# Two quads of value products in one turn, eight probability buffers, k over two turns, w_o and gate in one turn each

## The chip, the core and the metric

The kernel runs on one NeuronCore of one Trainium2 chip. The metric is device time in microseconds. The core has TensorE (PE in the profile; its weight loads are PEld), VectorE (DVE), ScalarE (ACT), GpSimd (POOL) and SyncE (SP), which here only issues DMAs.

## The reference

Sixteen sequences of 256 tokens by 256 features go through attention with 16 heads of 16 features, a layer norm over x plus attention, a mixture of 8 experts (two per token, capacity 1280 rows each, hidden size 1024) and a second layer norm:

```
q, k, v = x @ w.T, split in 16 heads
probs   = softmax(q k^T / 4)
x       = layernorm(x + (probs @ v) @ w_o.T)
gates   = softmax(x @ gating_w); top 2, weights normalised, dropped over capacity
x       = layernorm(x + sum over the two experts of weight * (relu(x @ w1 + b1) @ w2 + b2))
```

## The kernel before, in words

The program has three stages, one after the other: `attention` (lines 99 to 932), `experts` and `last_norm`. The change touches `attention` alone, which is the first 440 us or so.

In `attention` every engine walks the same list of turns, `for turn in range(LAST + 1)`, 182 of them. Each step has an offset in turns (lines 238 and 239), and `due(turn, offset, NB)` gives the sequence for which the step is due in this turn, if any; a sequence is started every 8 turns, so some seven sequences are in flight and a turn's content depends on turn mod 8, called its phase. `pair_of` gives the steps that are done in every turn, for one of the eight pairs of heads. Within a turn an engine does what is due in the order in which the code lists it, and waits on semaphores; nothing else keeps engines in step.

```
XT, Q, K, V, ST_IN, S0, MT, ST0, PV0 = 0, 2, 4, 8, 7, 12, 20, 23, 25
UT, AT, O, LN, X1, X1T, LG, CH, POS, LIST = 35, 37, 38, 41, 45, 46, 49, 54, 55, 59
```

TensorE (lines 822 to 932) does this in a turn, in this order: `scores` of a pair (line 787, four matmuls into the two banks SQ); `shifted_scores` of a pair (line 802, into SD); MT, transposes of the maxima; UT, eight transposes of unnormalised outputs (line 853); AT and X1T, transposes of attn and x1 (line 761); `pv` (line 818), the value products of one quad, that is four heads, with 128x32 tiles, sixteen matmul records; POS (lines 879 and 880); the q, k and v products, twelve matmuls each (helper line 752); O, the w_o product; LG, the gate product; XT, transposes of the next x. By phase, beside the eight matmuls of the two scores groups in each:

| phase | TensorE before |
|---|---|
| 0 | v product (12 matmuls), XT |
| 1 | one quad, half of the gate product (6) |
| 2 | q product (12), other half of the gate product (6) |
| 3 | UT, one quad |
| 4 | MT, k product (12) |
| 5 | AT, one quad |
| 6 | X1T, half of the w_o product (6) |
| 7 | one quad, POS, other half of the w_o product (6) |

VectorE's first work in a turn is the reduction of the scores to their negated maximum (line 672, `negm`); `scores` of the next turn waits for it, as SQ is held once. Behind it come, in the order of the code: `slots` (phase 0), `qk_lo` (line 570: q in phase 3, k in phase 5), `chosen` (lines 604 to 624, phase 6), layer norm statistics (phase 1), `heads_out` (lines 578 to 585, phase 3), mT_lo (phase 4), aT_lo (line 711, phase 5), y (line 718, phase 7), `largest` (lines 593 and 598, phase 2). ScalarE does first the exponential of a pair (line 488, `probs`), whose buffer is one of four; then by phase v_aug, mT_hi, x1 (line 519), aT_hi (line 526), x1T_f, `u_copy` of two quads (line 479, phases 3 and 7), xT_f and `qk_hi` (line 474: q in phase 2, k in phase 4). The w_o product waits for aT_lo (line 905).

The rows of q and k are then rearranged by six DMAs on SP's queue (lines 311 to 313) into `stack`, one of three buffers, from which `scores` reads from turn 12 of that sequence (phase 4) on. SP goes through its own list in order: in each sequence the four shift DMAs of line 291 (after mT_lo), two stores of x1 (lines 296 and 297, after x1), then the six of `stack`, after q_lo, k_lo and the use of that buffer three sequences back, then a load of x while there are sequences left. The scores of phase 4 wait for all six (line 782).

Before the turns, the weights are loaded into `w_raw` and transposed, and `ones_f` (two rows of ones) is copied into the stacks.

## Time and profile before

| | us |
|---|---|
| median of 3 runs | 980.37 |
| lowest and highest run | 977.14, 990.34 |
| the profiled execution, its own time | 981.65 |
| its span, first to last instruction | 979.8 |
| mean granted TensorE clock | 0.915 of full |
| PE, DVE, ACT, POOL busy in the span | 846.6, 561.8, 461.4, 431.8 |

Read it so: the time is that of the device, the span that of the profiled instructions, and all times of the rows below count from the span's start. Busy TensorE is an average over stages; what a turn costs is read from the starts of successive scores groups (line 787).

### The profile page before, as it was taken

The numbers are of one execution on the slowest core, as the hardware profiler recorded it, in microseconds if no ns is written. First come the engines' busy times: TensorE is split into PE (matmuls) and PEld (weight loads), VectorE is DVE, ScalarE is ACT, GpSimd is POOL, SyncE is SP. The second block draws the span as 40 slices with busy tenths as digits, with TensorE's granted clock in tenths as the row PEclk, the third lists the DMA queues.
The fourth block names the chain that finished last, engine by engine and source line by source line (L and its number), as shares of the span: only waits on it lengthen the run. The fifth ranks groups of instructions, "written<-read, shape, count | busy, mean of one in ns | idle before, by whom it ended". The sixth has DMA issues, their size and how long they took to land. (4 is left out here: it accounts for less than half of the span.)

```text
span 979.8 us, 19547 instructions
## 1 busy us (share of the span) xinstructions
PE 846.6 (86%) x7441; PEld 753.7 (77%) x7441; DVE 561.8 (57%) x1151; ACT 461.4 (47%) x851; POOL 431.8 (44%) x636
## 2 busy tenths in 40 slices
PE   5579889999999997840999999999999999999940
PEld 4466667677777765540999999999999999999940
DVE  3356647777777786241455666565555545666415
ACT  3036646666666665311344444444444444444316
POOL 2000215555656555474144545444444444545225
PEclk8579989999999999665899999999999999999985
DMA  5755967676775551014123444343442524322229
GB/s 127 101 80 79 246 126 117 106 119 115 116 113 97 90 108 28 23 44 152 34 45 87 88 91 87 48 95 84 93 87 43 130 45 86 87 44 46 26 35 334
DMA packets 74807, 90.75 MB, mean 93 GB/s; under 512 B 10428, under 2 KB 61788, under 8 KB 74588
## 3 DMA queue, kind: packets, MB, share of 16 engines
q1 hardware_dynamic: 57308, 68.47, 33.2%
q0 software_dynamic: 17408, 21.05, 13.2%
q8 instruction: 59, 0.97, 0.5%
q14 instruction: 32, 0.26, 0.1%
HBM read 37.87 MB, written 25.84 MB: 65 GB/s over the span
## 5 line engine op out<-in xcount | busy, mean ns | idle before, releaser
L1014 POOL DMA_INDIRECT acc_rows<-o_w,lists x80 | 136.5, 1706 | 242.0 <-ACT o_w L1065 229.8
L672 DVE TENSOR_REDUCE negm<-wide 128x4 f32<-128x1024 f32 x128 | 156.2, 1220 | 65.5 <-PE wide L787 65.3
L1143 PE MATMUL wide<-g_hi,w_hi 128*128 128x256 f32 x640 | 184.3, 288 | 0.0
L1145 PE MATMUL wide<-g_hi,w_lo 128*128 128x256 f32 x640 | 181.0, 283 | 0.0
L1144 PE MATMUL wide<-g_lo,w_hi 128*128 128x256 f32 x640 | 180.8, 282 | 0.0
L1162 PE MATMUL bank<-w_lo,h_hi 128*128 128x256 f32 x640 | 180.1, 281 | 0.0
L1161 PE MATMUL bank<-w_hi,h_hi 128*128 128x256 f32 x640 | 180.1, 281 | 0.0
L1163 PE MATMUL bank<-w_hi,h_lo 128*128 128x256 f32 x640 | 179.8, 281 | 0.0
L1055 ACT ACTIVATE h<-wide,b1T 128x256 f32<-128x256 f32 x320 | 132.9, 470 | 71.3 <-DVE h_hi L1098 53.2
L488 ACT ACTIVATE probs<-wide 128x1024 f32<-128x1024 f32 x128 | 131.0, 1024 | 74.0 <-PE wide L802 70.8
L1065 ACT ACTIVATE o_w<-o_b,lists 128x256 f32<-128x256 f32 x80 | 36.3, 502 | 193.6 <-DVE o_b L1111 193.6
L1143 PEld LDWEIGHTS wide<-g_hi,w_hi 128*128 128x128 f32 x640 | 121.5, 190 | 0.3 <-DVE g_lo L1088 0.3
L1144 PEld LDWEIGHTS wide<-g_lo,w_hi 128*128 128x128 f32 x640 | 121.6, 190 | 0.0
L1145 PEld LDWEIGHTS wide<-g_hi,w_lo 128*128 128x128 f32 x640 | 121.4, 190 | 0.0
L1161 PEld LDWEIGHTS bank<-w_hi,h_hi 128*128 128x128 f32 x640 | 120.5, 188 | 0.0
L1163 PEld LDWEIGHTS bank<-w_hi,h_lo 128*128 128x128 f32 x640 | 120.5, 188 | 0.0
L1162 PEld LDWEIGHTS bank<-w_lo,h_hi 128*128 128x128 f32 x640 | 120.4, 188 | 0.0
L1100 DVE TENSOR_TENSOR h_lo<-h,h_hi 128x512 fp32r<-128x512 f32 x160 | 110.7, 692 | 5.5
L1003 POOL DMA_INDIRECT rows<-x_rows,lists x80 | 88.2, 1102 | 33.2 <-issue 24.1
L1111 DVE TENSOR_TENSOR o_b<-bank,b_all 128x256 f32<-128x256 f32 x80 | 30.2, 419 | 113.9 <-PE bank L1163 113.9
L787 PE MATMUL wide<-stack 48*128 48x256 f32 x512 | 68.3, 347 | 25.2 <-DVE negm L672 16.0
L1098 DVE CAST h_hi<-h 128x512 fp32r<-128x512 f32 x160 | 70.1, 438 | 29.7 <-ACT h L1055 28.5
(162 smaller groups left out, 1510.4 us busy)
## 6 DMA issues: line engine op xcount, KB each, us to landing
stack<-qk SPq DMA_DIRECT2D x96, 256.0 KB, 8.1
w_raw<-in_L_ffn_w SPq DMA_DIRECT2D x16, 1024.0 KB, 5.9
x_sb<-in_L_attn_x SPq DMA_DIRECT2D x16, 256.0 KB, 8.6
x_rows<-x SPq DMA_DIRECT2D x16, 256.0 KB, 4.1
acc_rows<-x SPq DMA_DIRECT2D x16, 256.0 KB, 4.4
acc_sb<-acc_rows SPq DMA_DIRECT2D x8, 512.0 KB, 7.5
out<-out_sb SPq DMA_DIRECT2D x8, 512.0 KB, 3.7
x_rows<-zrow SPq DMA_DIRECT2D x1, 1280.0 KB, 11.8
```

The costliest lines, as they stand in the source:

```text
L488: nc.scalar.activation(probs[:, i % 4].rearrange("p x c t -> p x (c t)"), SD[:, :, :], ACT.Exp, scale=SCALE).then_inc(exp_done, 1)
L672: nc.vector.tensor_reduce(negm[n % 2][:, :, :, u].rearrange("p c x -> p x c"), SQ[:, :, :].rearrange("p x (c t) -> p x c t", c=QC), X, ALU ...
L1003: nc.gpsimd.indirect_dma_start(out=rows[c][:, r, :], out_offset=None, in_=x1_d, in_offset=bass.IndirectOffsetOnAxis(ap=lists[:, e, QC * c ...
L1014: nc.gpsimd.indirect_dma_start(out=acc_d, out_offset=bass.IndirectOffsetOnAxis(ap=lists[:, e, QC * c + r, 0:1], axis=0), in_=o_w[c][:, r, ...
L1055: ins = nc.scalar.activation(h[m % 2][:, i, :], bank(BZ[m], a=2)[:, i, :], ACT.Relu, bias=b1T[:, col:col + 1] if isinstance(col, int) else ...
L1100: nc.vector.tensor_tensor(h_lo[HBUF[c]][:, t, :], h[m % 2][:, :, :], h_hi[HBUF[c]][:, t, :].bitcast(F32), ALU.subtract).then_inc(h_lo_done, 1)
L1143: nc.tensor.matmul(out, w1_hi[:, k, f], G_hi[:, k, :], start=(k == 0), stop=False)
L1144: nc.tensor.matmul(out, w1_hi[:, k, f], G_lo[:, k, :], start=False, stop=False)
L1145: ins = nc.tensor.matmul(out, w1_lo[:, k, f], G_hi[:, k, :], start=False, stop=(k == DK - 1))
L1161: nc.tensor.matmul(out, H_hi[:, f, rs], w2_hi[:, f, :], start=(f == 0), stop=False)
L1162: nc.tensor.matmul(out, H_hi[:, f, rs], w2_lo[:, f, :], start=False, stop=False)
L1163: ins = nc.tensor.matmul(out, H_lo[:, f, rs], w2_hi[:, f, :], start=False, stop=(f == FT - 1))
```

## The change

It moves work between turns and makes `probs` larger. The value products of quads 0 and 1 are issued together in the turn in which quad 1 was due (phase 3), those of quads 2 and 3 in the turn of quad 3 (phase 7). `probs` gets eight buffers, one per pair, so the exponential of pair i waits for the value products of pair i - 8. The k product does its first six matmuls in phase 4 and the other six in phase 5; the ScalarE copy k_hi moves to phase 5 and the VectorE difference k_lo to phase 6. Both halves of the w_o product are issued in phase 6, both halves of the gate product in phase 1. The raw weights and the ones take no room of their own, they lie in buffers 4 to 7 of `probs`, which are first written by the exponentials of pairs 4 to 7. The number of instructions and all of their shapes stay.

```diff
--- before.py
+++ after.py
@@ -125,7 +125,10 @@
 
         tri = sb("tri", [P, P], BF16)
         ones = sb("ones", [P, P], BF16)
-        w_raw = sb("w_raw", [P, 4, DK, D])
+        probs = sb("probs", [P, PAIRS, 2, QC, S])
+        probs_flat = probs[:, :, :, :, :].rearrange("p u x c t -> p (u x c t)")
+        w_raw = probs_flat[:, 4 * 4 * S:4 * 4 * S + 4 * DK * D].rearrange("p (w c d) -> p w c d", w=4, c=DK)
+        ones_f = probs_flat[0:2, 6 * 4 * S:6 * 4 * S + PAIRS * S].rearrange("p (u t) -> p u t", u=PAIRS)
         wT_hi = sb("wT_hi", [P, 4, DK, D], F32R)
         wT_lo = sb("wT_lo", [P, 4, DK, D], F32R)
         b1_raw = sb("b1_raw", [NE * FT, P])
@@ -135,7 +138,6 @@
         iota_e = sb("iota_e", [P, NE])
         fill = sb("fill", [P, NE, BLK, 2], I32)
         zrow = sb("zrow", [P, D])
-        ones_f = sb("ones_f", [2, PAIRS, S])
         tok = sb("tok", [P, QC])
 
         x_sb = [sb(f"x_sb{i}", [P, QC, D]) for i in range(XB)]
@@ -149,7 +151,6 @@
         negm = [sb(f"negm{i}", [P, QC, 2, PAIRS]) for i in range(2)]
         mT_hi = sb("mT_hi", [H, S], F32R)
         mT_lo = sb("mT_lo", [H, S], F32R)
-        probs = sb("probs", [P, 4, 2, QC, S])
         u_sb = sb("u_sb", [P, QUADS, S])
         rec = sb("rec", [P, QC, H])
         attn = sb("attn", [P, QC, D])
@@ -483,9 +484,9 @@
                 if p is not None:
                     i = PAIRS * p[0] + p[1]
                     act.wait_ge(st_ready, i + 1)
-                    if i >= 4:
-                        act.wait_ge(pv_ready, (i - 4) // 2 + 1)
-                    nc.scalar.activation(probs[:, i % 4].rearrange("p x c t -> p x (c t)"), SD[:, :, :], ACT.Exp,
+                    if i >= PAIRS:
+                        act.wait_ge(pv_ready, (i - PAIRS) // 2 + 1)
+                    nc.scalar.activation(probs[:, i % PAIRS].rearrange("p x c t -> p x (c t)"), SD[:, :, :], ACT.Exp,
                                          scale=SCALE).then_inc(exp_done, 1)
                 m = due(turn, CH, NB)
                 if m is not None:
@@ -545,7 +546,7 @@
                 n = due(turn, Q, NB)
                 if n is not None:
                     qk_hi(n, 0, q_ready, q_hi_done)
-                n = due(turn, K, NB)
+                n = due(turn, K + 1, NB)
                 if n is not None:
                     qk_hi(n, 1, k_ready, k_hi_done)
 
@@ -681,7 +682,7 @@
                 n = due(turn, Q + 1, NB)
                 if n is not None:
                     qk_lo(n, 0, q_hi_done, q_lo_done)
-                n = due(turn, K + 1, NB)
+                n = due(turn, K + 2, NB)
                 if n is not None:
                     qk_lo(n, 1, k_hi_done, k_lo_done)
                 m = due(turn, CH, NB)
@@ -761,9 +762,9 @@
                         ins = nc.tensor.transpose(banks[bk][:, c * S + r * P:c * S + r * P + P], src[:, r, c * P:c * P + P], ident[:, :])
                 return ins
 
-            def by_feature_tile(w, n):
+            def by_feature_tile(w, n, tiles=range(G)):
                 hi, lo = xT_hi[n % 2], xT_lo[n % 2]
-                for o in range(G):
+                for o in tiles:
                     ins = product(banks[BC][:, o * S:o * S + S], split_pairs(
                         lambda i: wT_hi[:, w, i, o * P:o * P + P], lambda i: wT_lo[:, w, i, o * P:o * P + P],
                         lambda i: hi[:, i, :], lambda i: lo[:, i, :]))
@@ -815,7 +816,7 @@
                     for j in range(4):
                         u = 2 * t + j // 2
                         out = banks[BU][32 * j:32 * j + 32, (t % 2) * S:(t % 2) * S + S]
-                        ins = nc.tensor.matmul(out, v_aug[n % VB][:, c, 4 * t + j, :], probs[:, u % 4, j % 2, c, :],
+                        ins = nc.tensor.matmul(out, v_aug[n % VB][:, c, 4 * t + j, :], probs[:, u, j % 2, c, :],
                                                start=(c == 0), stop=(c == QC - 1), tile_position=(0, 32 * j))
                 ins.then_inc(pv_ready, 1)
 
@@ -865,10 +866,11 @@
                     pe.wait_ge(attn_done, min(m + 2, NB))
                     pe.wait_ge(x1T_lo_done, m)
                     transpose4(BB, x1[m % 2]).then_inc(x1T_ready, 1)
-                for t in range(QUADS):
-                    m = due(turn, PV0 + 2 * t, NB)
+                for half in range(2):
+                    m = due(turn, PV0 + 2 + 4 * half, NB)
                     if m is not None:
-                        pv(m, t)
+                        pv(m, 2 * half)
+                        pv(m, 2 * half + 1)
                 m = due(turn, POS, NB)
                 if m is not None:
                     pe.wait_ge(seen_done, m + 1)
@@ -888,7 +890,10 @@
                 if n is not None:
                     pe.wait_ge(q_lo_done, n + 1)
                     pe.wait_ge(wT_lo_done, 2)
-                    by_feature_tile(1, n).then_inc(k_ready, 1)
+                    by_feature_tile(1, n, (0,))
+                n = due(turn, K + 1, NB)
+                if n is not None:
+                    by_feature_tile(1, n, (1,)).then_inc(k_ready, 1)
                 n = due(turn, V, NB)
                 if n is not None:
                     if n >= 2:
@@ -904,11 +909,9 @@
                 if m is not None:
                     pe.wait_ge(aT_lo_done, m + 1)
                     by_row_tile(BA, aT_hi, aT_lo, 3, 0)
-                m = due(turn, O + 1, NB)
-                if m is not None:
                     by_row_tile(BA, aT_hi, aT_lo, 3, 1).then_inc(o_ready, 1)
                 for c in range(QC):
-                    m = due(turn, LG + c, NB)
+                    m = due(turn, LG, NB)
                     if m is not None:
                         if c == 0:
                             pe.wait_ge(x1T_lo_done, m + 1)
```

## Rows read from the trace of the kernel before

**Rows 1.** Windows view, 240 to 260 us: busy us (instructions) by engine, clock, DMA.
```profile
240.00:260.00 20.00, 18.98 (x192) 14.69 (x191) 14.88 (x31) 12.34 (x19) 11.79 (x28) 1.00 0.68 115
```

**Rows 2.** Timeline of TensorE: start, us, engine, line, operation, tiles, count [idle before <-releaser].
```profile
141.71 0.51 PE L787 MATMUL wide<-stack 48*128 48x256 f32 x4
...
243.82 0.50 PE L787 MATMUL wide<-stack 48*128 48x256 f32 x4
...
246.31 0.50 PE L787 MATMUL wide<-stack 48*128 48x256 f32 x4
...
248.50 0.22 PE L752 MATMUL bank<-gate_hi,x1T_hi 128*128 128x128 f32 x1
...
249.21 0.50 PE L787 MATMUL wide<-stack 48*128 48x256 f32 x4
...
250.13 1.06 PE L853 MATMUL bank<-ident,u_sb 128*128 128x128 f32 x8 [0.18 <-DVE ix L598]
...
251.13 1.07 PE L818 MATMUL bank<-probs,v_aug 128*32 128x256 f32 x16
...
252.13 0.50 PE L787 MATMUL wide<-stack 48*128 48x256 f32 x4
...
253.21 0.36 PE L752 MATMUL bank<-xT_hi,wT_hi 128*128 128x256 f32 x1
253.41 0.28 PE L752 MATMUL bank<-xT_lo,wT_hi 128*128 128x256 f32 x1
...
254.81 0.50 PE L787 MATMUL wide<-stack 48*128 48x256 f32 x4
...
258.85 0.39 PE L752 MATMUL bank<-wT_hi,aT_hi 128*128 128x256 f32 x1 [0.47 <-DVE aT_lo L711]
...
259.98 0.50 PE L787 MATMUL wide<-stack 48*128 48x256 f32 x4 [0.15 <-DVE negm L672]
...
262.67 0.51 PE L787 MATMUL wide<-stack 48*128 48x256 f32 x4
...
273.89 0.50 PE L787 MATMUL wide<-stack 48*128 48x256 f32 x4
...
339.99 0.50 PE L787 MATMUL wide<-stack 48*128 48x256 f32 x4
```

**Rows 3.** Timeline of VectorE, 256 to 262 us, the columns as above.
```profile
256.49 0.68 DVE L570 TENSOR_TENSOR qk<-bank,qk 128x512 fp32r<-128x512 f32 x1
258.10 0.69 DVE L711 TENSOR_TENSOR aT_lo<-bank,aT_hi 128x512 fp32r<-128x512 f32 x1 [0.93 <-ACT aT_hi L526]
258.71 1.22 DVE L672 TENSOR_REDUCE negm<-wide 128x4 f32<-128x1024 f32 x1
...
261.36 1.21 DVE L672 TENSOR_REDUCE negm<-wide 128x4 f32<-128x1024 f32 x1
```

**Rows 4.** Timeline of SP's DMA issues of three stack loads.
```profile
58.47 0.63 SPq L311 DMA_DIRECT2D stack<-qk  x1
...
192.60 0.64 SPq L311 DMA_DIRECT2D stack<-qk  x1
...
258.61 0.64 SPq L311 DMA_DIRECT2D stack<-qk  x1
...
263.54 0.61 SPq L313 DMA_DIRECT2D stack<-qk  x1
```

**Rows 5.** Line 313 in 55 to 66 us, and its issue at 263.54.
```profile
DMA to landing us min/median/max: 6.6/7.6/8.6
...
DMA to landing us min/median/max: 10.2/10.2/10.2
```

**Rows 6.** Timeline of TensorE, phase 4 scores that waited for the load of 192.60.
```profile
208.84 0.51 PE L787 MATMUL wide<-stack 48*128 48x256 f32 x4 [0.92 <-DMA stack<-qk]
```

**Rows 7.** Windows view, 78 to 82 us, columns as in rows 1.
```profile
78.00:80.00 2.00, 0.99 (x12) 0.65 (x16) 1.40 (x2) 0.92 (x1) 0.00 (x0) 1.00 0.19 52
80.00:82.00 2.00, 2.00 (x20) 0.75 (x20) 0.71 (x1) 1.09 (x2) 0.00 (x0) 0.50 1.04 188
```

## The prediction

> **What bounds the kernel now.** I read the page's slices first, to see which part of the span the change touches: the first 440 us, where attention runs. A window of steady turns shows TensorE working 18.98 of 20 us at the full clock, VectorE 14.88, ScalarE 12.34 [rows 1]. Then the timeline of TensorE over one sequence: eight turns, each opened by a scores group; 141.71 to 339.99 is nine sequences, 22.03 us each [rows 2]. Inside, TensorE is back to back but for 0.18 us (for DVE ix), 0.47 (for aT_lo) and 0.15 (for negm). So order of TensorE's work decides, with two chains beside it. One is ScalarE to VectorE in phase 5 (phase = turn mod 8): aT_hi, aT_lo, then the next reduction [rows 3]. The other is the stack load: k_lo on VectorE, six issues on SP, landing, scores of phase 4. It is the nearest to the edge: issues begin at 258.61, the last of them (263.54) lands 10.2 us later, at 273.74 [rows 4, 5], while phase 4 of the next sequence comes at 273.89, one clean period (21.76 us) after 252.13. Once it is late: scores waited 0.92 us at 208.84 [rows 6]. I take T0..T7 for the scores' start in phases 0 to 7.
>
> **The change, phase by phase** (clean period, all from [rows 2] unless named).
> - Value products. One quad takes 1.00 us (251.13 to 252.13). Phases 1 and 5 lose one, phases 3 and 7 gain one; no instruction is removed. The exp values that they read are two or more turns old with eight buffers, so no new wait on exp; the ScalarE copy of the pair begins about one turn's end later, and the bank is not needed for four turns.
> - Gate products. Phase 2 loses its six: 249.21 minus 248.50 = 0.71. Phase 1 gains them: 2.49 - 1.00 + 0.71 = 2.20 (-0.29). Phase 2: -0.71. VectorE reads the logits in phase 2 as before but no longer has to wait for them, so ix is early and the 0.18 us wait in phase 3 goes: +1.00 - 0.18 = +0.82 there.
> - k projection. Twelve matmuls take 1.60 us (253.21 to 254.81). From the second on (253.41) they take 0.127 each, the first 0.20: a second half costs 0.80 + 0.08. Phase 4: -0.72, to 1.96 us. VectorE's floor for a turn is scores 0.50, reduction 1.22 and semaphores, some 1.85, so this turn stays just above it. The 0.08 lies between 0 and 0.2 (the whole first matmul); I take what the two cadences give.
> - Phases 5 and 6. Phase 5 gives up 1.00 for 0.88. But T5 + 4.04 is when the w_o product may begin (258.85), since ScalarE does exp, x1 and aT_hi in that order and aT_lo ends only at 258.79 [rows 3]. Nothing in that chain moves: k_hi, now in phase 5, is ScalarE's last item of the turn. Twelve w_o matmuls instead of six (1.60, as k's twelve) end at T5 + 5.64; before, T7 was T5 + 5.17. So +0.47: the gap before w_o cannot be filled, and what stands behind it has grown.
> - Phase 7. It loses six w_o matmuls (0.89 = half of 1.60 plus 0.09) and gains a quad, +0.11. VectorE: k_lo (0.60 net of overlap) now stands between the reduction of 258.71 and `chosen`, so the next reduction starts at T5 + 6.55 + 0.60 = 7.15, ends 8.36, and scores T0 can't come before T5 + 8.5, against 8.44 by TensorE: +0.05.
> - The sum of a clean period: -0.29 - 0.71 + 0.82 - 0.72 + 0.47 + 0.11 + 0.05 = -0.27 us; nine of them, -2.4 us.
>
> **The stack load.** k_lo is issued one turn later and stands behind aT_lo and the reduction of phase 6: it ends at T5 + 5.12 + 0.60, SP issues at about T5 + 5.77, that is T4 + 7.7 (1.96 + 5.77). Before it was T4 + 6.48 (258.61 - 252.13). SP's own queue ahead (four shift DMAs, two x1 stores) is done by then, so the delay is 1.2 us. First issue to landing took 13.6 us where no x1 store ran (58.47, last issue 5.0 later, 8.6 to land), 15.1 (258.61 to 273.74), and 16.2 at the worst (192.60 to 208.84) [rows 4 to 6]. With stores finished before the load begins I take 0.7 us off the latter two (half of the way to 13.6 for the shorter); the bounds are 0 and 1.5. Then phase 4 comes at T4 + 7.7 + 13.6 = 21.3 (hidden under the 21.5 of TensorE), with 14.4 at 22.1 (0.6 late), with 15.5 at 23.2 (1.7 late). For nine loads I estimate one of 1.7 and four around 0.35, 3.1 us together, in place of the 0.92 of before: +2.2 us. Nine periods together: -0.2 us.
>
> **Start and end.** In the last two passes there is no q, k or v product: phases 2 and 4 sit on VectorE's floor and cannot give their 0.71 and 0.72 back, while phase 3 still pays 1.00 and phases 5 and 6 about 0.5 against 0.3 gained in phase 1: +1.2 or 1.3 each, +2.5. At the start two k halves run under reductions at half clock (about 1.4 us each gained), but the load chain with its added 1.2 us per sequence takes it back, and after the one long stop of this stage a pair of quads instead of one runs at half clock: +0.6 net, bounds -2 and +4. Weights and ones now lie inside `probs`: read before the fifth exp, nothing waits, 0.
>
> Sum: -0.2 + 2.5 + 0.6 = +2.9 us on 981.65 (the profiled execution; 979.8 its span) = 984.6. This execution lies 1.3 us above the median of the three runs, so against 980.37 the forecast is 983.3 us. Two per cent (19.6 us) is about what can be told from no change.
>
> **Two rules of the Trainium skill.** TensorE takes 0.20 us for the first k matmul and 0.127 for the following ones [rows 2]. The Trainium skill ("TensorEngine Tiling (Array Packing)", Key Properties) says that changing the tiling mode drains the engine; value products use 128x32 tiles, and the change drops two such visits per sequence. By the row each visit saves some 0.1 us, which is -3 us in all, and my sum doesn't count it; the rule has the same sign. The second speaks against the change. At 78 to 80 us TensorE was busy 0.99 of 2 us, and in the next 2 us its granted clock was 0.50 [rows 7]. The Trainium skill ("TensorE: Matmul & The Clock Gate", HAM oscillation) says that waits for a DMA between bursts of matmuls bring the slow clock back each time; the trace agrees here, while the 0.92 us wait of [rows 6] was not enough. It is the second half of rival C.
>
> **Rivals.**
> - A: the load is never late and the pairs of quads save their switches. For it: 13.6 us without stores. Against: 15.1 and 16.2. Time: 983.3 - 3.1 - 3.0 = 977.2.
> - B: stores were not what made the load long; it is late in most periods. 7.7 + 14.8 = 22.5 against 21.5: 1.0 x 9 = 9 in place of 3.1: 989.2. For it: 15.1 in the steady period with an x load in it as well, which stays.
> - C, slower than before: the load becomes the bound and the clock falls with it. Place: scores in phase 4. k_lo would have to land the load 1.7 us late in each period (a mean of 15.5 us from issue), and the pause then lets the clock fall to half for some 2.6 us, 1.3 us lost. 1.7 + 1.3 - 0.3 = 2.7 per period, x 9 = 24, plus 2.9 - (-0.2) of start and end: 980.4 + 24 + 3 = 1007. It decides from about 15.2 us of loading on. Against: only one load in nine was that long, and TensorE has 19 of 20 us of work.
> - D, faster by over 2%: 2.2 us a period would have to go; all waits of TensorE (0.8) and the late load (0.1 on average) are 0.9. No rule or row gives it.
>
> **Chances.** Forecast 0.48, A 0.22, B 0.21, C 0.07, D 0.02. Faster by over 2%: 0.02 (D). Slower: 0.07 (C). Within: 0.91. The range reaches from A (977) with 1 us below it to B with three falls of the clock (989 + 3 x 1.3 = 993) and the upper bound of the start: 976 to 995.
>
> **What would show it.** In a steady sequence: T4 to T5 about 1.95; T5 to T7 5.6 with still 0.4 to 0.5 us waiting for aT_lo ahead of the w_o product; T3 to T4 3.7; two value groups back to back; first qk issue 7.7 after T4; more and longer waits of the phase-4 scores for stack. The period 21.5 to 22.2. Wrong if the clean period is below 21.2 or above 22.5, if TensorE waits in phases 0 to 3, if the stack load is late by more than 1 us in most sequences, or if the stage after 440 us changes at all.

## The result and the profile after

| | before | after |
|---|---|---|
| median (runs), us | 980.30 (4) | 993.38 (4) |
| lowest, highest | 977.14, 990.34 | 989.08, 996.28 |
| the profiled execution, its span | 981.65, 979.8 | 991.66, 989.7 |
| mean granted TensorE clock | 0.915 | 0.914 |

The ratio is 1.0176, with an interval of 1.0124 to 1.0228. It is not the quotient of the two medians, which is 1.0133; in the table of the experiments the two differ by up to 0.4 points (`a_o_apart`), so a few tenths of a per cent rest on neither alone. The same changed kernel was compared twice more, with 12 runs against 29 each time: 990.16 against 990.78 (0.9978, 0.9948 to 1.0009) and 990.60 against 986.41 (1.0068, 1.0031 to 1.0105). The changed kernel stands at 990 to 993 in all three; it is the kernel before that moved, from 980 to 991, and where the chip is known it moved with it: 990.78 and 990.76 in two groups of runs on one chip, 986.41 and 986.62 on another, 985.36 on a third. The three intervals do not overlap, so an interval from one comparison understates the spread between chips. What follows reads the difference as somewhere from nothing to 1.8%, and takes its places from the traces. Only one trace of the kernel before is kept, of the execution of 981.65 us, and none of those at 985 to 991 us that stand beside the experiments: a reading against it says where two executions differ, not where two medians do.

The two profiled executions differ by 9.9 us of span. The scores groups date it. Timeline of TensorE after (columns as in [rows 2]; the scores are line 788 now, the value products 819):

```profile
29.82 0.80 PE L788 MATMUL wide<-stack 48*128 48x256 f32 x4 [8.70 <-issue]
...
52.63 0.80 PE L788 MATMUL wide<-stack 48*128 48x256 f32 x4 [0.29 <-DVE negm L673]
...
73.83 0.50 PE L788 MATMUL wide<-stack 48*128 48x256 f32 x4
...
145.47 0.50 PE L788 MATMUL wide<-stack 48*128 48x256 f32 x4
...
167.69 0.50 PE L788 MATMUL wide<-stack 48*128 48x256 f32 x4 [1.14 <-DMA stack<-qk]
...
169.52 0.50 PE L788 MATMUL wide<-stack 48*128 48x256 f32 x4
...
173.56 0.38 PE L753 MATMUL bank<-wT_hi,aT_hi 128*128 128x256 f32 x1 [0.55 <-DVE aT_lo L712]
...
178.40 0.74 PE L803 MATMUL wide<-stack 50*128 50x256 f32 x4 [2.72 <-DMA stack<-mT_lo]
179.07 1.08 PE L819 MATMUL bank<-probs,v_aug 128*32 128x256 f32 x8
...
193.25 0.50 PE L788 MATMUL wide<-stack 48*128 48x256 f32 x4
...
299.84 0.85 PE L819 MATMUL bank<-probs,v_aug 128*32 128x256 f32 x12
301.71 0.50 PE L788 MATMUL wide<-stack 48*128 48x256 f32 x4
...
303.54 0.51 PE L788 MATMUL wide<-stack 48*128 48x256 f32 x4
...
305.51 0.51 PE L788 MATMUL wide<-stack 48*128 48x256 f32 x4
...
309.21 0.51 PE L788 MATMUL wide<-stack 48*128 48x256 f32 x4
...
311.97 0.50 PE L788 MATMUL wide<-stack 48*128 48x256 f32 x4
...
314.74 0.50 PE L788 MATMUL wide<-stack 48*128 48x256 f32 x4
...
316.89 0.51 PE L788 MATMUL wide<-stack 48*128 48x256 f32 x4
...
322.92 0.50 PE L788 MATMUL wide<-stack 48*128 48x256 f32 x4
...
344.34 0.50 PE L788 MATMUL wide<-stack 48*128 48x256 f32 x4 [0.32 <-DMA stack<-qk]
```

The scores of turn 12 begin within 0.05 us of before (29.87), those of turn 52 at 145.47 against 141.71 [rows 2]: +3.8 us. Nine sequences then take 198.87 against 198.28: +0.6. From there to the last shifted scores (408.18 before, 415.20 after) it is +2.7, and to the last write of `slot_list` (starts 446.69 and 455.68) +2.0 more; the remaining 0.9 us lies in the 534 us behind it, which the change does not touch.

One clean sequence is 301.71 to 322.92, 21.2 us (21.76 before); the best were 21.10. The turns opened from 301.71 to 316.89 are phases 4 to 2 of it. Two quads back to back take 299.84 to 301.71, 1.87 us. The windows view of both kernels (columns as in [rows 1]), after first:

```profile
50.00:70.00 20.00, 15.79 (x86) 13.26 (x86) 10.34 (x11) 6.22 (x9) 1.88 (x2) 0.55 0.61 89
70.00:90.00 20.00, 17.13 (x152) 11.13 (x150) 10.09 (x10) 10.31 (x14) 0.97 (x2) 0.76 0.52 80
200.00:360.00 160.00, 151.49 (x1595) 118.47 (x1596) 122.83 (x271) 102.15 (x155) 90.63 (x205) 1.00 0.69 112
```

```profile
50.00:70.00 20.00, 14.72 (x100) 11.82 (x100) 11.18 (x11) 6.65 (x10) 1.89 (x2) 0.68 0.56 81
70.00:90.00 20.00, 18.25 (x185) 13.00 (x185) 11.54 (x12) 12.40 (x18) 1.89 (x2) 0.91 0.64 95
200.00:360.00 160.00, 151.57 (x1570) 114.35 (x1568) 121.80 (x269) 101.70 (x153) 92.57 (x222) 1.00 0.68 109
```

Two things are to be seen. In the steady stage, 200 to 360 us, the engines did about the same work at the same full clock. At the start, 50 to 90 us, the granted clock was 0.55 and 0.76 against 0.68 and 0.91, and TensorE ran 238 matmul records where it had run 285.

The start can be followed turn by turn. At first the changed kernel is ahead: turns 12 and 20, without half of k, take 2.30 and 1.83 us where they took 3.58 and 3.82, and the scores of turn 21 begin at 52.63 us against 55.99. Then its clock stays at half from about 52 to 73 us, where before it was full from 56 to 59 us and again from 66 us on, and at turn 28 it is behind (73.83 against 72.87). Turn 31 adds 2.6 us and turn 43 adds 1.4. The long stop in turn 47 costs nothing extra (10.38 us for 10.69). Why the clock came back later is open.

What a half clock costs depends on what stands there. Timeline of TensorE after, then before, in turn 31, where the clock falls in both:

```profile
79.34 0.69 PE L788 MATMUL wide<-stack 48*128 48x256 f32 x4 [1.09 <-DVE negm L673]
80.48 0.80 PE L803 MATMUL wide<-stack 50*128 50x256 f32 x4 [0.45 <-DMA stack<-mT_lo]
81.21 1.08 PE L819 MATMUL bank<-probs,v_aug 128*32 128x256 f32 x8
84.78 0.80 PE L788 MATMUL wide<-stack 48*128 48x256 f32 x4
```

```profile
55.99 0.54 PE L787 MATMUL wide<-stack 48*128 48x256 f32 x4
...
72.87 0.51 PE L787 MATMUL wide<-stack 48*128 48x256 f32 x4 [0.18 <-DVE negm L672]
...
78.94 0.50 PE L787 MATMUL wide<-stack 48*128 48x256 f32 x4 [1.09 <-DVE negm L672]
...
79.95 1.08 PE L818 MATMUL bank<-probs,v_aug 128*32 128x256 f32 x8
81.81 0.79 PE L787 MATMUL wide<-stack 48*128 48x256 f32 x4
```

The pair of quads (81.21 to 84.78) takes 3.6 us, the single quad 1.9: the merged turn is caught whole. Its scores also began 0.4 us later and the shifted scores waited 0.45 us for the shifted maxima.

The third place is the one slow sequence among the nine, 167.69 to 193.25, 25.56 us. The scores of 167.69 waited 1.14 us for `stack`; then, at 178.40, the shifted scores waited 2.72 us for `mT_lo`, and the pair behind took 3.31 us at half clock. SP's list around it:

```profile
172.41 0.63 SPq L292 DMA_DIRECT2D stack<-mT_lo  x1
...
175.32 0.64 SPq L312 DMA_DIRECT2D stack<-qk  x1
```

The last shift DMA was issued at 172.41 and landed at 178.40, 6 us later. First `qk` issue at 175.32 is 167.69 + 7.63. The same sequence took 25.91 and 25.72 us in the two repeats of this kernel, with a wait for `stack` (0.97, 0.96) before it each time, so it is no accident of one execution.

### The profile page after: what moved, and what is told of

It reads as the page before. It is cut to its first block and busy times, and to the rows that moved or that the text cites. A ratio compares the mean times of both kernels' runs of the same rounds, so it can differ in the third digit from the quotient of the medians.

```text
span 989.7 us, 19543 instructions
## 1 busy us (share of the span) xinstructions
PE 844.1 (85%) x7441; PEld 759.1 (77%) x7441; DVE 561.5 (57%) x1151; ACT 459.7 (46%) x851; POOL 432.8 (44%) x636
```

## The experiments

Every kernel ran beside the kernel before on the same chip; kernels of one group share its runs. Group 1 ran on one chip, groups 2 and 5 on a second, 3 and 4 on a third. The expectations name their explanations by letters: L, the late stack load; P, the pairs of value products; O, the whole w_o product behind aT_lo; M, a late load that costs only together with the shorter phases of the change.

| group | kernel | median | before | ratio, 95% interval |
|---|---|---|---|---|
| 1 | a_k_whole | 992.09 | 985.36 | 1.0056, 1.0022 to 1.0090 |
| 1 | a_pv_apart | 990.70 | 985.36 | 1.0032, 1.0004 to 1.0061 |
| 1 | a_o_apart | 998.37 | 985.36 | 1.0092, 1.0059 to 1.0125 |
| 1 | a_klo_first | 983.73 | 985.36 | 0.9972, 0.9941 to 1.0003 |
| 2 | after_again | 990.16 | 990.78 | 0.9978, 0.9948 to 1.0009 |
| 2 | b_late_load | 994.65 | 990.78 | 1.0027, 0.9988 to 1.0066 |
| 2 | b_pv_pairs | 1035.19 | 990.78 | 1.0446, 1.0394 to 1.0499 |
| 2 | b_o_gate | 982.48 | 990.78 | 0.9915, 0.9880 to 0.9951 |
| 3 | after_third | 990.60 | 986.41 | 1.0068, 1.0031 to 1.0105 |
| 3 | a_klo_again | 982.57 | 986.41 | 0.9963, 0.9931 to 0.9995 |
| 3 | b_o_gate_again | 978.70 | 986.41 | 0.9924, 0.9888 to 0.9960 |
| 3 | a_pv_apart_klo | 998.15 | 986.41 | 1.0103, 1.0039 to 1.0167 |
| 4 | b_pv_fill | 1017.24 | 986.62 | 1.0302, 1.0250 to 1.0355 |
| 4 | b_pv_k | 1008.48 | 986.62 | 1.0203, 1.0155 to 1.0250 |
| 4 | b_o | 979.60 | 986.62 | 0.9923, 0.9895 to 0.9951 |
| 4 | b_gate | 987.72 | 986.62 | 0.9999, 0.9962 to 1.0036 |
| 5 | b_k_halves | 996.17 | 990.76 | 1.0043, 1.0006 to 1.0080 |
| 5 | h_mix | 983.87 | 990.76 | 0.9925, 0.9895 to 0.9955 |

**One part of the change undone.** `a_k_whole` computes k whole in phase 4 again, with k_hi and k_lo in their old turns:

```diff
-                    by_feature_tile(1, n, (0,))
-                n = due(turn, K + 1, NB)
-                if n is not None:
-                    by_feature_tile(1, n, (1,)).then_inc(k_ready, 1)
+                    by_feature_tile(1, n).then_inc(k_ready, 1)
```

> The changed kernel with the k product whole in phase 4 again (k_hi in phase 4, k_lo in phase 5). Theory L (the stack load begins 1.2 us later because of the k halves, TensorE waits for it and its clock falls): 983 us or less, about 10 of the 13 us come back, first stack issue about 6.5 us after the scores of phase 4, waits for stack below 1 us in all, and the start of the stage (scores of turn 52 at about 142 us instead of 145.5). Theory P (the pairs of value products cost it, by long phases 3 and 7): 992 to 995, hardly changed. Theory O (w_o whole behind aT_lo costs it): hardly changed.

Theory L is refuted as it was put: 992 us, not 983. The waits for `stack` shrank to two in the nine sequences, 0.26 and 0.33 us, and the slow sequence at 167 us went. But the kernel was no faster: another sequence took 25.07 us. It had waits of 0.5, 0.4 and 1.18 us in phases 5 and 6 (237 to 240 us), where the k half had been, and the clock was at half from 240 to 246. Removing the late load alone doesn't pay if its turn is left thin.

`a_pv_apart` issues one quad every second turn as before:

```diff
-                for half in range(2):
-                    m = due(turn, PV0 + 2 + 4 * half, NB)
+                for t in range(QUADS):
+                    m = due(turn, PV0 + 2 * t, NB)
                     if m is not None:
-                        pv(m, 2 * half)
-                        pv(m, 2 * half + 1)
+                        pv(m, t)
```

> The changed kernel with the value products of each quad in its own turn again (eight probability buffers stay). Theory L: 990 to 996, no gain, since the load stays late. Theory P: 983 or less. By the sum of my prediction the quads in phases 1 and 5 would add work ahead of nothing and the clean period grows by 0.1 to 0.3 us, some 2 us in all, while the end of the stage gets 1 to 2 us shorter.

It took 990.70 us, as theory L said, at a ratio of 1.0032. Three loads were late among the nine sequences (0.71, 0.57 and 0.22 us), and phase 5, with a quad and a k half, took 3.16 us. This group has no run of the changed kernel itself, so what the pairs do within the change is not told closer than by the 990 to 993 us of that kernel elsewhere: hardly anything.

`a_o_apart` moves the second half of the w_o product back to phase 7:

```diff
                     by_row_tile(BA, aT_hi, aT_lo, 3, 0)
+                m = due(turn, O + 1, NB)
+                if m is not None:
                     by_row_tile(BA, aT_hi, aT_lo, 3, 1).then_inc(o_ready, 1)
```

> The changed kernel with the second half of the w_o product in phase 7 again. Theory O: 985 or less, because phases 5 and 6 fall back from 5.6 to 5.2 us. Theory L or P: 992 to 998; by my sum T5 to T7 becomes 5.2 us but phase 7 grows by 0.9, so the clean period grows by 0.4 us, +4 us in all.

It was the slowest of the group, 7.7 us above `a_pv_apart` by the medians (0.6 points by the ratios): the merged w_o product, which I had priced at a small loss (+0.47 in phases 5 and 6, -0.89 in a phase 7 that the quad filled again), looks like a gain.

`a_klo_first` keeps the whole change, and moves only VectorE's k_lo from the next turn to right behind aT_lo in phase 5:

```diff
-                n = due(turn, K + 2, NB)
-                if n is not None:
-                    qk_lo(n, 1, k_hi_done, k_lo_done)
...
+                n = due(turn, K + 1, NB)
+                if n is not None:
+                    qk_lo(n, 1, k_hi_done, k_lo_done)
                 m = due(turn, O + 1, NB)
```

> The changed kernel with k_lo computed right behind aT_lo at the end of phase 5 instead of behind the reduction of phase 6. Theory L: the load begins 1.1 to 1.2 us earlier, waits for stack become rare, 984 to 988 us. Theories P and O: 993, plus 1 us because the reduction of phase 6 begins 0.6 us later and holds up the scores of phase 7 by 0.1 us.

Its first issue in the second of the sequences below is at 169.68, 6.5 us after the scores of phase 4 (163.18), as in the kernel before. Timeline of TensorE of `a_klo_first`, to be read beside that of after:

```profile
142.10 0.50 PE L788 MATMUL wide<-stack 48*128 48x256 f32 x4
...
163.18 0.50 PE L788 MATMUL wide<-stack 48*128 48x256 f32 x4
...
170.78 0.51 PE L788 MATMUL wide<-stack 48*128 48x256 f32 x4
...
184.27 0.50 PE L788 MATMUL wide<-stack 48*128 48x256 f32 x4
...
334.48 0.50 PE L788 MATMUL wide<-stack 48*128 48x256 f32 x4
```

The sequence that took 25.56 us takes 21.09 (163.18 to 184.27), the shifted scores of 170.78's turn no longer wait, and the nine take 192.38 us, 6.5 less than after. One single wait for `stack` of 0.31 us is left among them. It was 8.4 us below `a_k_whole`. Against the kernel before it is 0.3% lower, which the interval does not part from nothing, and `a_klo_again` gave 0.4%:

> The changed kernel with k_lo right behind aT_lo, again, on the same chip as the changed kernel itself. Theory L: 5 to 9 us below the changed kernel (0.991 to 0.995 of it), nine steady periods of 21.1 to 21.4 us each. If the load is not what costs: within 2 us of it.

Its nine sequences took 195.18 us where the changed kernel of the same group took 201.82, and the medians are 982.57 and 990.60 us, as theory L said. So the late k_lo costs 8.0 us, 0.8%, far more than the 3 to 4 us for which the scores waited for `stack` in the traces of the changed kernel. The edit moves k_lo on VectorE and the load together, and with it the slow sequence goes. Whether the load makes the shift DMA slow is another question: `b_pv_pairs` below has the slow shift without a late load.

**Parts of the change alone.** The same kernel once more, and three parts on the kernel before:

> The changed kernel itself, on the chip of its neighbours, as their yardstick. 1.2 to 2 per cent above before; mean granted clock at or below 0.912 against 0.917 of before if the falls of the clock are part of the loss, with 6 to 7 us for each 0.01.

> The changed kernel a third time, beside before on one chip. If its loss of the first comparison (1.0176) was its own: 1.012 to 1.023 of before. If the change is worth nothing by itself and the first comparison caught before in few falls of the clock: 0.995 to 1.005, with the same mean granted clock in both within 0.003.

A loss of 1.2 per cent or more did not come back on either chip (0.9978 and 1.0068), and the mean clocks, 0.917 and 0.916, were those of the kernel before (0.915 and 0.918). Nine sequences took 202.22 and 201.82 us in their profiles.

`b_late_load` leaves the kernel before as it is and holds the six `stack` issues back to where the change has them:

```diff
                     sp.wait_ge(k_lo_done, n + 1)
+                    if n >= 1:
+                        sp.wait_ge(max_done, PAIRS * n - 5)
```

> The kernel before, where SP waits also for the reduction of phase 6 before it issues the six stack loads, and nothing else is changed: the load alone begins later (about 7.6 us after the scores of phase 4 instead of 6.5). Theory L: slower by 7 to 12 us than before, waits for stack of 0.3 to 1.8 us in most sequences. If the load is only late together with the shorter phases of the changed kernel (theory M, a mixture): slower by 0 to 4 us.

The loads came late in six sequences (up to 1.77 us at 92.31), two of them among the nine (0.31 and 0.24 us). The ratio is 1.0027, which the interval does not part from nothing: theory M, not L. Its trace is less mild. The nine sequences took 210.52 us, and three of them 26.34, 25.44 and 25.73 us at a granted clock of 0.87. In the first of these the shifted scores waited 1.45 us for `mT_lo` (0.84 before). The other two had no late load; VectorE and ScalarE began late in their phase 5, of which more below, and phase 6 took 3.96 and 4.37 us instead of 2.92. Without a trace of the kernel before on this chip, what of this is the edit's stays open.

`b_pv_pairs` has the eight buffers and the pairs of quads, and nothing else of the change:

```diff
-                for t in range(QUADS):
-                    m = due(turn, PV0 + 2 * t, NB)
+                for half in range(2):
+                    m = due(turn, PV0 + 2 + 4 * half, NB)
```

> The kernel before with eight probability buffers and the value products in pairs, k, w_o and gate products as before. Theory L: within 3 us of before. Theory P, now as: pairs leave phases 1 and 5 thin, TensorE waits there for VectorE and its clock falls: slower by 4 to 8 us, mean clock down by 0.005 or more, no waits for stack.

It costs 4.5%, 44 us where theory P had 4 to 8, the largest effect of the study, and no wait for `stack` is in its nine sequences. Windows view, and the timeline of TensorE in one sequence with the one reduction of VectorE ahead of it (280.78 opens phase 5, 283.38 phase 6, 287.59 phase 7):

```profile
200.00:360.00 160.00, 142.54 (x1310) 106.06 (x1306) 100.34 (x218) 85.80 (x130) 78.05 (x177) 0.89 0.54 90
```

```profile
280.78 0.50 PE L788 MATMUL wide<-stack 48*128 48x256 f32 x4
282.10 1.23 DVE L673 TENSOR_REDUCE negm<-wide 128x4 f32<-128x1024 f32 x1 [1.22 <-PE wide L788]
283.38 0.50 PE L788 MATMUL wide<-stack 48*128 48x256 f32 x4 [1.27 <-issue]
...
284.90 0.66 PE L762 MATMUL bank<-ident,x 128*128 128x128 f32 x4 [0.47 <-ACT x L520]
286.11 0.49 PE L753 MATMUL bank<-wT_hi,aT_hi 128*128 128x256 f32 x1 [0.55 <-DVE aT_lo L712]
...
287.59 0.80 PE L788 MATMUL wide<-stack 48*128 48x256 f32 x4
288.75 1.06 PE L819 MATMUL bank<-probs,v_aug 128*32 128x256 f32 x8
```

With the quad gone from phase 5, nothing covers ScalarE's and VectorE's chain: 1.27, 0.47 and 0.55 us of idle time within the 4.0 us up to 286.11. Of the 1.27 us about 0.8 are no matter of the order: the reduction of phase 5 began 1.32 us after its scores, where 0.55 is usual. At 286 the matmul records grow from 0.28 to 0.42 us, the half clock; the scores take 0.80 and the pair 2.35 us. From the second of the nine sequences on each takes 25.4 to 28.2 us, and the mean clock of the 160 us is 0.89, busy time 142.5 us of 160 where before had 151.6. The first of the nine, with the reduction on time (0.54 us) and the full clock, took 22.85 us for the 21.67 of before: that much goes with the order of the work. The Trainium skill ("TensorE: Matmul & The Clock Gate", A second HAM failure mode) says that short idle times between groups of matmuls can make the clock swing between its two levels, without any long wait; this trace agrees.

The second of the nine, 28.23 us, has the slow shift of the changed kernel without its late load. The timeline of SP, then of TensorE:

```profile
175.93 0.63 SPq L292 DMA_DIRECT2D stack<-mT_lo  x1
...
177.75 0.64 SPq L312 DMA_DIRECT2D stack<-qk  x1
```

```profile
182.05 0.80 PE L803 MATMUL wide<-stack 50*128 50x256 f32 x4 [2.74 <-DMA stack<-mT_lo]
```

The load was issued 6.5 us after the scores of phase 4 (171.22), as in the kernel before, and still the shifted scores waited 2.74 us, for a shift DMA issued 6.1 us earlier. `b_pv_fill` and `b_pv_k` have the same there (2.68 and 2.30 us, sequences of 28.23 and 27.53 us). With a late load and the quads apart the wait is shorter (1.04 us in `a_pv_apart`, 1.45 in `b_late_load`), and with pairs and an early load it is missing in `a_k_whole` and `a_klo_first`. So neither the late load nor the pairs alone decide it, and what does stays open.

To part the idle time from its effect on the clock, `b_pv_fill` does the four transposes of attn in phase 5 three times, which adds work and leaves the output as it is:

```diff
-                    transpose4(BA, attn).then_inc(aT_ready, 1)
+                    transpose4(BA, attn)
+                    transpose4(BA, attn)
+                    transpose4(BA, attn).then_inc(aT_ready, 1)
```

> The kernel before with value products in pairs and eight buffers, as b_pv_pairs, and the four transposes of attn in phase 5 done three times over (the same values to the same place, eight transposes of work that nobody needs, about 0.9 us a sequence). Clock theory (phase 5 is too thin, TensorE idles and its clock falls in nearly every sequence): faster than b_pv_pairs by 20 us or more although it does more, 0.995 to 1.02 of before, mean clock above 0.905. If the pairs cost by themselves (buffers, order, waits of the copies): 1.045 or more.

```profile
200.00:360.00 160.00, 145.25 (x1457) 111.67 (x1457) 107.90 (x234) 92.51 (x140) 80.75 (x180) 0.99 0.60 100
```

More work in less time: 3.0% over before instead of 4.5%, though less than the clock theory had said. The clock is back at 0.99 in the window, sequences take 24.04 to 24.08 us from the fourth on, and the nine take 220.92 us for 235.62. The two kernels ran on different chips, each beside the kernel before; the traces, 14.7 us apart in these nine, say the same as the ratios. So of the 4.5% some 1.5 points are the clock. The rest is the turns: phase 7, with a pair and half of w_o, takes 3.5 us where it had 2.7 and phase 3 3.8 for 2.9, while phase 1, which gave its quad away, only falls from 2.5 to the 1.83 us that VectorE's reduction allows. Phase 6 takes 3.87 us for 2.92, although its work on TensorE is as before; here the reduction of phase 5 is still late (1.2 us), and that part of the cost is not explained.

`b_pv_k` adds the k halves to `b_pv_pairs` (with k_hi and k_lo a turn later, as in the change):

```diff
+                n = due(turn, K + 1, NB)
+                if n is not None:
+                    by_feature_tile(1, n, (1,)).then_inc(k_ready, 1)
```

> The kernel before with pairs of quads, eight buffers and k in halves, w_o and gate as before. Clock theory: the half of k (0.88 us) fills phase 5 as the idle work does: 1.00 to 1.02 of before and near the changed kernel. Otherwise 1.04 or more.

The half product does for phase 5 what the filler did (clock 0.99 in the same window), and takes itself from phase 4, whose turn drops from 2.43 to 1.83 us. A clean sequence is 22.6 us. The ratio of 1.0203 is at the upper edge of what was expected, and further from the changed kernel than was said. On the kernel before, without the pairs, the same halves cost 0.4%:

> The kernel before with only k in halves (k_hi in phase 5, k_lo in phase 6). By my sum: phase 4 -0.72, phase 5 +0.88, the reductions behind aT_lo later; the load 1.2 us later: 1.003 to 1.012 of before, waits for stack in several sequences.

`b_o_gate` has only the two lines that merge the w_o and the gate product, `b_o` and `b_gate` one each:

```diff
-                m = due(turn, O + 1, NB)
-                if m is not None:
                     by_row_tile(BA, aT_hi, aT_lo, 3, 1).then_inc(o_ready, 1)
-                    m = due(turn, LG + c, NB)
+                    m = due(turn, LG, NB)
```

> The kernel before with w_o whole in phase 6 and the gate product whole in phase 1. By my prediction's sum: phases 5 and 6 +0.87 (w_o ends at T5 + 5.6 and the pair of waits stays), phase 7 -0.89, phases 1 to 3 -0.2: 980 to 984 where before is 985 (-1 to -5 us), no change of the load. Theory O: slower than before by 4 us or more.

> The kernel before with w_o whole in phase 6 and the gate product whole in phase 1, again: 0.988 to 0.995 of before, 5 to 12 us below it, if the 0.9915 of the first comparison was its own.

> The kernel before with only the w_o product whole in phase 6. If w_o brings the gain of b_o_gate (one switch less, a longer burst, y earlier): 0.990 to 0.995 of before. If the gate does: 0.998 to 1.003.

> The kernel before with only the gate product whole in phase 1. If the gate brings the gain of b_o_gate (the 0.18 us wait for ix and one late 0.09 go): 0.990 to 0.996 of before; by my sum -0.2 to -0.3 us a period, 0.996 to 0.998.

The gain, 8 us where the sum had 1 to 5, is all w_o's: 0.8% with it, nothing by the gate product alone. Clean sequences are no shorter (21.76 in `b_o`). One place can be shown, in the start. Timeline of TensorE of `b_o_gate`, then of before, at the longest stop of the start:

```profile
125.39 0.80 PE L802 MATMUL wide<-stack 50*128 50x256 f32 x4 [4.92 <-DMA stack<-mT_lo]
126.11 1.08 PE L818 MATMUL bank<-probs,v_aug 128*32 128x256 f32 x8
127.98 0.79 PE L787 MATMUL wide<-stack 48*128 48x256 f32 x4
```

```profile
126.10 0.80 PE L802 MATMUL wide<-stack 50*128 50x256 f32 x4 [6.02 <-DMA stack<-mT_lo]
126.83 1.08 PE L818 MATMUL bank<-probs,v_aug 128*32 128x256 f32 x8
...
130.27 0.79 PE L787 MATMUL wide<-stack 48*128 48x256 f32 x4
```

After a stop of 5 to 6 us the clock is at half, and whatever is next runs at that rate. Before, that was a quad and half of w_o (126.83 to 130.27); with w_o done ahead of the stop it is the quad alone (126.11 to 127.98), 1.6 us less. Turns 12 to 52 took 109.58 us in `b_o` and 111.84 before, but 108.95 in `b_gate`, whose median is no lower than before: a shorter start in one execution is no proof of a gain. Where the 7 to 8 us between the medians come from, the traces do not say.

**Two combinations.** `a_pv_apart_klo` is `a_klo_first` with the quads apart:

> The changed kernel with the quads apart again and k_lo right behind aT_lo: k halves, w_o and gate merged, early load. If pairs of quads are worth nothing once k fills phase 5 and the load is early: within 2 us of the changed kernel with k_lo early. Theory P (pairs leave phases thin and the clock falls): 3 to 8 us below it, the fastest of the four. If pairs help by their saved visits (0.2 to 0.4 us a period): 3 to 5 us above it.

It lost 1.4% against `a_klo_again` of the same group, 15.6 us by the medians and more than any of the theories had said. A quad and a k half together make phase 5 3.16 us long and push phase 6 to 4.05, so the clean sequence is 22.3 us for 21.1. Three of the nine took 25.5 to 25.6 us, with 4.86 us in a phase 0 of 2.77. So with a k half in phase 5 and k_lo early the pairs are right, though alone on the kernel before they cost 4.5%; with k_lo late (`a_pv_apart`) they made hardly a difference.

`h_mix` keeps w_o and gate merged throughout, uses whole k products for the first six sequences and single quads for the first four, and `a_klo_first`'s form from there:

```diff
+                    if m is not None and m < 4:
+                        pv(m, t)
+                    if m is not None and m >= 4 and t % 2 == 1:
+                        pv(m, t - 1)
+                        pv(m, t)
```

> A mixture: w_o and gate whole throughout; the first six k products whole and the first four sequences' quads apart; from then on k in halves with k_lo right behind aT_lo, and quads in pairs. If the first stretch and the steady one keep what b_o_gate and a_klo_again gained there (turn 52 at about 139 us, steady periods of 21.1): 972 to 978 us where before is 986, 0.985 to 0.991 of before. If the gains don't combine: 0.992 to 0.997.

Its nine sequences took 195.36 us, the clean ones 21.08 to 21.10, and 983.87 against 990.76 is 0.7% less than before: level with `b_o_gate` (0.8%), which is the simpler kernel and the one to keep. The two gains did not combine, as the second half of the expectation has it.

## Why the prediction was right or wrong

The forecast was 983.3 us, +2.9 on before; the first comparison gave 993.4, +13.1. The median lies near the upper end of the range of 976 to 995; the ratio of 1.0176 on 980.37 would be 997.6, outside it. The forecast was too low, and by its steps:

- **Phases.** Medians over the nine sequences, before to after: phase 1 2.48 to 2.16 (-0.29 forecast), phase 2 2.91 to 2.29 (-0.71), phase 4 2.59 to 1.83 (to 1.96), phases 5 and 6 5.17 to 5.65 (5.64), phase 7 +0.08 (+0.11), phase 3 2.92 to 3.56 where no load was late (+0.82 forecast, +0.64 measured). Phase 0 was forecast at +0.05 and fell by 0.16. A clean sequence was 0.5 to 0.6 us shorter, not 0.27. This part held, and what I missed in it was in the kernel's favour; the cleanest sequence, 21.10 us, is just below the 21.2 at which I had called the account wrong.
- **The switches of tile mode.** A pair takes 1.87 us where two quads took 2 x 1.00: 0.13 us a pair. The row of k's first matmul had suggested 0.1. The rule on draining (the Trainium skill, "TensorEngine Tiling (Array Packing)", Key Properties) agrees in sign and this row has its size; it is part of why the clean sequence came out shorter.
- **The load.** The first issue came 7.63 us after T4 (7.7 forecast). The nine waited 1.14, 0.79, 0.56, 0.29 and 0.32 us: 3.1 us together, the sum that I had estimated. The w_o product began at T5 + 4.04, as forecast.
- **The step that failed: the late load priced at its waits alone, "3.1 us together, in place of the 0.92 of before: +2.2 us".** The waits were right and the price was not. With clean sequences 0.5 to 0.6 us shorter (about 5 us in nine) and 2.2 us more of waits, the nine should have come out 2.8 us shorter. They were 0.6 us longer, so some 3.4 us came on top. They are in the one sequence of 25.56 us, 4.4 more than a clean one, where the last shift DMA landed 6 us after its issue, the shifted scores waited 2.72 us and the pair behind them ran at half clock. I had left such an effect to rival C, at 7 in 100 and only for loads 1.7 us late in each sequence. Measured on one chip, moving k_lo back to the end of phase 5 gave 8.0 us (990.60 to 982.57) and took the slow sequence away. So the late k_lo costs 8.0 us where I had +2.2. That its late load is what makes the shift slow is not shown, since `b_pv_pairs` has that shift with the load on time: the way from the one to the other stays open.
- **The term most mis-sized: the start.** +0.6 with bounds of -2 and +4 was +3.8. The gain of the k halves came, larger than I had it (1.3 us in turn 12, 2.0 in turn 20, for 1.4 each); the load's delay is not what took it back. The clock stayed at half longer (0.55 and 0.76 in the two windows), and between turns 21 and 28 a lead of 3.4 us became a delay of 1.0. The pair at half clock, which I had named, costs 1.7 us in turn 31 (3.64 for 1.93). Behind the long stop it takes 3.10 us, but there the half of w_o that stood behind the quad is gone, and the turn is no longer than before.
- **The end.** +2.5 was +2.7 to the last shifted scores, and another +2.0 behind them on the way to the last list.
- **The level.** These four terms (3.8, 0.6, 2.7 and 2.0) make 9.1 of the 9.9 us between the profiled executions. The other part of the miss is the reference: the kernel before ran at 980 in the first comparison and at 985 to 991 on the chips of all later ones. By those, the change is -0.2% or +0.7%, and the forecast's +0.3% lies between them.
- **The rivals.** A (load never late) is refuted for the change, and `a_klo_first` shows what it would have been: 0.3 to 0.4% faster, near A's 977 against 980. B was right on five late loads of nine, but not on their size. C had a fall of the clock behind a wait, which came in one sequence of nine instead of each, and behind the wait for the shift and not the one for the load. Its 2.6 us of half clock stand in no row; the fall at 80 us in [rows 7] lasted longer (0.50 over 2 us, 0.65 over the next 2). None of them had the effect that `b_pv_pairs` shows: alone the pairs cost 4.5%, and the other parts are what makes them bearable (with the k halves +2.0% in `b_pv_k`, with w_o and gate merged +0.6% in `a_k_whole`). I had priced each part with the cover of all the others in place.
- **A row misread.** The idle time ahead of the fall at 80 us in [rows 7] was a wait of 1.09 us for VectorE's reduction (78.94) and not one for a DMA, so it is no case of the rule that I set beside it. The DMA case in that trace is the stop of 6.02 us at 126.10, behind which the quad ran at half clock.

Taken apart, the parts are: pairs +4.5%, k halves +0.4%, w_o -0.8%, gate 0. They do not add up (pairs, k halves and gate are +0.9% in `a_o_apart`, the whole is between -0.2 and +1.8%): each fills a turn that another has thinned.

One thing stays open. In `b_pv_pairs` and `b_pv_fill` VectorE's reduction began 1.2 to 1.4 us after the scores of phase 5 where 0.55 is usual, from the third of the nine sequences on, and ScalarE's work was equally late, with ordinary matmul records ahead of it and the clock full. It is not the pairs' own: single sequences of `b_late_load` (0.86 us, the sequences of 25.44 and 25.73 us), `b_o` (0.96) and `b_o_gate` (1.17) have it too, and the traces of the first comparison, before and after, have it in none of their nine. What sets it no run shows, and it is an untested rival to the order of the work wherever a trace of the later groups is read against that of before.

## What to carry to other kernels

In a pipeline written out by turns, price a moved product by what it leaves behind as well: a turn that falls below the other engines' chain turns its saving into idle pieces, and a few of these in a row also take the clock. When an input is issued later, do not price its own wait alone: undo just that step on the same chip, look for other waits that come or go with it, and ask which instructions would run at half clock after them; a merged block is the worst thing to have there. Compare on one chip, as the kernel before differed by 0.5% between two (985.36 and 990.78). Undo and add single parts in both directions before a bundle is judged, since here the best result (0.8%) was one part of a bundle that as a whole was a loss or nothing.

## What was not expected of the hardware

- The time of an execution goes with its mean granted clock. Over the 29 runs of before in group 1 (977.9 to 992.4 us) each 0.01 of mean clock went with 6.7 us, correlation -0.90; other kernels gave 3.7 to 11.6 us, at correlations of -0.45 to -0.97. For this kernel most of the spread from run to run goes with the clock; what makes it fall more often in one run than in another is not shown.
- Idle pieces of 1.27, 0.47 and 0.55 us within 4 us came before a fall to half in `b_pv_pairs`, while the single wait of 1.14 us at 167.69 did not bring one on the spot: the scores behind it took 0.50 us, as at the full clock (0.80 at half). A wait of 1.09 us was followed by one in turn 31, so the length of a wait alone does not tell.
- Eight more transposes a sequence on the busiest engine made a kernel faster, by 1.4 points of its ratio (`b_pv_fill` against `b_pv_pairs`).
